# Five per-token stages as two merged half-batch chunks, context keys made once, expert rows added in DRAM

## The chip, the core and the metric

The kernel runs on one core of a Trainium2 chip. The metric is the device time of one execution in microseconds (us), as the median of several runs. Engines: PE is TensorE, DVE is VectorE, ACT is ScalarE, POOL is GpSimd, SP is SyncE, which issues nearly all DMAs. Each engine runs its own static list of instructions, and semaphores join them.

## The reference

The input is x (4 batches, 1024 tokens, 256 wide) and a context of 77 rows per batch. Eight stages follow, each added to x, most after a layer norm:

```
L0 attention on the context (differential, two softmaxes), then L0 block:
   own causal attention (16 heads of 16), then the best 2 of 8 experts per token
   (256 -> 1024, gelu, 1024 -> 256), weighted by a softmax over the two gates
C1 attention on the context, 16 heads of 16, with output projection
L1 ternary weights, 8-bit activations:
   xq = clip(round(x * (127 / max|x|)));  gelu(xq @ W1q.T + b1) quantised again, @ W2q.T + b2
D2 attention on the context, with biases and output projection
L2 butterfly block:  x @ W_exp, butterfly (linear), + bias, gelu, butterfly, @ W_con
E3 attention on the context, some context rows masked, no output projection
F3 a router takes 4 of 16 heads (64 wide) by the mean of all 1024 tokens of the batch,
   self attention with these, output projection
```

C1, L1, D2, L2 and E3 work on each token alone (the 77 context rows are fixed for a batch). F3 needs all tokens of a batch.

## The kernel before

Everything lives on one core in four parts. A **preamble** splits weights into high and low float16 halves and multiplies the butterfly factors into two dense matrices. **Phase 0** runs batches 0 to 3 unrolled through L0 attention, own attention and the gate; at its end POOL notes each token's place in the experts' table (L1595). **Phase 1** runs the experts in 23 tiles of 512 gathered rows. POOL gathers the normalised rows of a tile (L1610), the tile's results are stored in order to `scr_expert_rows`, and `final_slots` on DVE (L2079 to L2088) works out for every token where its two results lie. Then `add_expert_rows` on POOL (L1617) gathers 16 times 128 rows and adds them to `h_tokens` (L1622). **Phase 2** is a loop of four passes, one per batch (`Fori` at L673 on SP, L1112 on PE, L1464 on ACT, L1632 on POOL, L2130 on DVE). A pass first makes the context keys KX and values VX of its batch for C1, D2 and E3 (ACT L1470/L1473, DVE L2138/L2140), then does C1, L1, D2, L2, E3 and F3 one after the other, each over all 1024 tokens, and POOL adds the next batch's expert rows in the middle of the pass.

The order of the work inside an attention is a hand-written list, `context_attention_steps` (L115; `unprojected_steps` L146 for E3), which every engine walks through: S scores to find the row maximum (PE L923, DVE L1886), MT maxima turned (PE L934), ST scores turned with the maximum subtracted (PE L948) and exponentials on ACT (L1357), PV products with the values and a row of ones (PE L965), RINV and NB for the inverse sums, output projection in three parts WS, WB, WL (`split3` L763 to L765, three matmuls for one product in split float16). The path has several trips by DMA: the queries go to `scr_q` and come back as `q_stack` (L563, L568), the maxima as rows (L541), the sums of the probabilities out to another layout and, inverted on DVE (L1909), back (L548, L550), after which NB (L978) spreads them with a matmul and DVE multiplies (L1913). The ternary stage has per 128 tokens a matmul up (L1138, L1142), `hidden` on DVE (L2170), gelu on ACT (L1487), `quantise` on DVE (L2176 to L2190) with ACT L1493, transposes and ACT L1498, a matmul down (L1150, L1155) and two operations on DVE (L2194, L2197). The butterfly stage has L1174 up, gelu on ACT (L1513), L1183 down. `claim()` gives a matmul one of the PSUM slots: A0, A1 (large), B0, B1, S0, S1.

Of the kernel before, what the change touches and what calls it, by code (L numbers as in the profile page):

```python
# [7 lines left out]
P = 128  # L8
# [20 lines left out]
NP, NPX = 5, 7  # L29
# [10 lines left out]
FLAT = ["A0q", "A0o", "B0q", "B0k", "B0v", "C1q", "D2q", "E3q"]  # L40
PADDED = ["B0p", "C1o", "D2o", "F3o"]
# [73 lines left out]
def context_attention_steps():  # L115

    def S(g, a, b):
        return [("S", g, t) for t in range(a, b)]

    def ST(g, a, b):  # L120
        return [("ST", g, 0, j) for j in range(a, b)]

    def PV(g):
        return [("PV", g, 0, 0), ("PV", g, 0, 1)]

    steps = S(0, 0, NT) + [("MT", 0)] + S(1, 0, NT) + [("MT", 1)]
    for j in range(GH):
        steps += ST(0, j, j + 1) + S(2, 2 * j, 2 * j + 2)
    steps += [("MT", 2)]
    for g in range(NG):  # L130
        for j in range(GH if g + 1 < NG else 0):
            if j == 3:
                steps += PV(g)
            steps += ST(g + 1, j, j + 1) + (S(3, 2 * j, 2 * j + 2) if g == 0 else [])
        if g == 0:
            steps += [("MT", 3)]
        if g == NG - 1:
            steps += [("WS", 0)] + PV(g)
        else:
            steps += [("RINV", g)]  # L140
        if g:
            steps += [("NB", g - 1)]
    return steps + [("RINV", NG - 1), ("WS", 1), ("WB", 0), ("WB", 1), ("NB", NG - 1), ("WS", 2), ("WB", 2), ("WL",)]


def unprojected_steps():  # L146

    steps = [("TO", s[1]) if s[0] == "NB" else s for s in context_attention_steps()]
    return [s for s in steps if s[0] not in ("RINV", "WS", "WB", "WL")]


def attention_steps(L, route=False):
    if L == "E3":
        return unprojected_steps()
    return own_attention_steps(route) if L == "B0" else context_attention_steps()
# [24 lines left out]
def build(nc, A, out, known, stages):  # L180
    led = Ledger(known)
    with ExitStack() as ctx:
# [55 lines left out]
        maskr = sb("mask_row", [1, TX], I32)  # L238
# [6 lines left out]
        def area(kb, n, dt=F32, rows=P):  # L245
# [5 lines left out]
        stage_pad = area(32, len(PADDED) * PAD_N)  # L251
# [8 lines left out]
        kxs = area(40, 2 * 3 * KD * TX, F16).rearrange("p (s l k c) -> p s l k c", s=2, l=3, k=KD)  # L260
        kxf = area(44, 3 * KD * TX).rearrange("p (l k c) -> p l k c", l=3, k=KD)
        CT = area(47, 2 * KD * TX, F16).rearrange("p (s k c) -> p s k c", s=2, k=KD)
        maskb = area(56.5, NH * TX, F16, rows=1).rearrange("p (h c) -> p h c", h=NH)
        tmp = area(60, T)
        XN = {k: area(o, NT * D).rearrange("p (t d) -> p t d", d=D) for k, o in
              {"A": 48, "B": 16, "M": 38, "C": 16, "D": 16, "E": 16, "L1": 16, "L2": 16, "F": 28}.items()}
        VP = area(0, NT * NH * QUARTER).rearrange("p (t h d) -> p t h d", h=NH, d=QUARTER)
        PR = area(16, NP * T).rearrange("p (n c) -> p n c", c=T)
        PRX = area(8, NPX * T).rearrange("p (n c) -> p n c", c=T)
        OT = {True: [area(36 + 4 * (g % 2), T) for g in range(NG)],  # L270
              False: [area(36, T), area(40, T), area(0, T), area(4, T)]}
# [38 lines left out]
        slots_u = area(63.5, 2 * NT * NB).bitcast(U32)  # L310
# [6 lines left out]

        b1b = area(0, HID)
        hb = area(4, 3 * HID).rearrange("p (n c) -> p n c", n=3)
        xq = area(24, NT * D, F16).rearrange("p (t d) -> p t d", d=D)  # L320
        xqT = area(28, KD * T, F16).rearrange("p (k c) -> p k c", k=KD)
        hq = area(32, 2 * HID, F16).rearrange("p (n c) -> p n c", n=2)
        hqT = area(36, 2 * HID, F16).rearrange("p (n c) -> p n c", n=2)
        b2b = area(40, D)
        hr = area(44, 2 * HID).rearrange("p (n c) -> p n c", n=2)

        XTf = area(0, KD * T).rearrange("p (k c) -> p k c", k=KD)
        gT = area(24, 2 * NM * CH).rearrange("p (n m c) -> p n m c", n=2, m=NM)

# [2078 lines left out]
```

## Time and profile before

| what | value |
|---|---|
| median of 3 runs | 4590.6 us (4576.54, 4590.60, 4591.11) |
| profiled execution | 4634.11 us, its span 4632.3 us |
| busy, share of the span | PE 72%, DVE 52%, PE weight loads 39%, ACT 31%, POOL 8% |
| mean granted TensorE clock | 0.808 of full speed |
| phase 2 begins | 2210.7 us |
| passes | four |

The profiled execution is one run; the windows and timelines below have its time, counted from the start of its span. Busy time of an engine counts its instructions, without the issue of DMAs and waits for semaphores. The granted clock is that of TensorE alone, as a fraction of 2.4 GHz. In a timeline, the number in brackets is how long the engine was idle before the row, and what ended the idle time; "x16" is sixteen instructions in a row.

### The profile page before, as it was taken

Reading aid. Unit: us, or ns where it says so; the run is one execution under the profiler, and the core shown is the slowest. Engines: PE = TensorE matmul, PEld = TensorE weight load, DVE = VectorE, ACT = ScalarE, POOL = GpSimd, SP = SyncE. Lnnn points to the kernel's source line nnn. Section 1 sums busy time; section 2 is a strip of 40 time slices with the busy share of each in tenths; the row PEclk is TensorE's granted clock in tenths of the full one; section 3 lists DMA queues with packets and bytes.
Section 4 is the critical chain, followed back from the end, with each engine's and each line's share of the span. In section 5 each row is a group of like instructions: output and inputs, shape, how many; then the busy total and the mean of one; then the engine's idle time right before and its main releaser. Section 6 shows DMA issues by size and latency. Waiting matters only on the chain.

```text
span 4632.3 us, 49203 instructions
## 1 busy us (share of the span) xinstructions
PE 3357.5 (72%) x18898; PEld 1800.3 (39%) x18898; DVE 2394.3 (52%) x4963; ACT 1452.2 (31%) x2041; POOL 370.6 (8%) x287
## 2 busy tenths in 40 slices
PE   5278677677677579997558596585966777856769
PEld 2132332332332256675335333353333453433524
DVE  8765465465465345554563443634437434365343
ACT  2234433433333323332242323332224332233222
POOL 6000001001001112112020000200002000020000
PEclk7677777777768889998769797687887788877889
DMA  3210311311221044443320303201131112131110
GB/s 123 98 38 15 120 33 15 109 44 15 92 61 15 29 160 140 139 137 100 59 48 5 72 2 67 50 10 31 46 65 36 25 24 53 42 58 26 24 53 24
DMA packets 186166, 266.56 MB, mean 58 GB/s; under 512 B 86985, under 2 KB 132570, under 8 KB 173530
## 3 DMA queue, kind: packets, MB, share of 16 engines
q1 hardware_dynamic: 167934, 240.61, 19.1%
q0 software_dynamic: 17984, 22.63, 2.8%
q8 instruction: 157, 2.57, 0.2%
q14 instruction: 91, 0.75, 0.1%
HBM read 185.37 MB, written 75.33 MB: 56 GB/s over the span
## 4 chain that ended last, share of the span: by engine, by line
PE 52%; DVE 27%; DMA 8%; ACT 5%; issue 4%; SPq 2%; another core or an unknown queue 1%; POOL 1%; DVEq 0%; ACTq 0%; POOLq 0%
PE ps L763 6%; PE ps L764 5%; PE ps L765 5%; PE ps L965 5%; PE ps L1251 4%; PE ps L948 4%; DVE max_parts L1880 4%; PE ps L910 3%; PE ps L1174 2%; PE ps L1183 2%; DVE minus_max L1886 2%; PE ps L978 2%; DMA q_stack<-scr_q 2%; DVE arena L1799 2%; ACT arena L1357 2%
## 5 line engine op out<-in xcount | busy, mean ns | idle before, releaser
L1357 ACT ACTIVATE arena<-ps 104x1024 f32<-104x1024 f32 (+8 forms) x704 | 514.1, 752 | 838.0 <-PE ps L948 602.1
L1880 DVE TENSOR_REDUCE max_parts<-ps 128x1 f32<-128x512 f32 (+3 forms) x768 | 389.3, 552 | 258.4 <-PE ps L913 160.3
L910 PE MATMUL ps<-k_stack,q_stack 96*128 96x512 f16 (+3 forms) x768 | 277.4, 397 | 94.1 <-DVE max_parts L1880 50.3
L1797 DVE CAST arena<-arena 128x512 f16<-128x512 f32 (+2 forms) x304 | 161.5, 531 | 332.4 <-ACT arena L1440 222.6
L948 PE MATMUL ps<-q_stack,k_stack 98*128 98x512 f16 (+3 forms) x768 | 265.3, 393 | 37.2 <-ACT arena L1357 22.8
L1622 POOL DMA_INDIRECT h_tokens<-scr_expert_rows,slots_of_batch x80 | 127.0, 1587 | 1915.6 <-DMA slots_of_batch<-scr_slots 1832.2
L1799 DVE TENSOR_TENSOR arena<-arena 128x512 f16<-128x512 f32 (+2 forms) x304 | 274.5, 903 | 10.4
L763 PE MATMUL ps<-arena 128*128 128x256 f16 (+2 forms) x824 | 223.0, 275 | 72.0 <-DVE arena L2133 70.6
L2273 DVE TENSOR_REDUCE max_parts<-ps 128x1 f32<-128x512 f32 x256 | 171.4, 689 | 184.5 <-PE ps L1226 182.4
L1251 PE MATMUL ps<-arena 128*96 128x512 f32 x512 | 246.1, 592 | 1.7 <-ACT arena L1558 1.7
L1558 ACT ACTIVATE arena<-ps 128x1024 f32<-128x1024 f32 x128 | 130.5, 1023 | 345.8 <-PE ps L1240 345.8
L821 PE MATMUL ps<-identf,arena 128*128 128x128 f32 x512 | 114.6, 415 | 170.2 <-DVE arena L1780 170.2
L1440 ACT ACTIVATE arena<-ps,arena 128x512 f32<-128x512 f32 x184 | 126.4, 687 | 355.2 <-PE ps L765 311.1
L764 PE MATMUL ps<-arena 128*128 128x256 f16 (+2 forms) x824 | 223.7, 274 | 0.0
L765 PE MATMUL ps<-arena 128*128 128x256 f16 (+2 forms) x824 | 223.3, 274 | 0.0
L910 PEld LDWEIGHTS ps<-k_stack,q_stack 96*128 96x128 f16 x768 | 77.3, 104 | 337.6 <-DVE max_parts L1880 247.9
L763 PE MATMUL ps<-x_channels_hi_lo,arena 128*128 128x512 f16 x432 | 168.4, 390 | 52.7 <-DVE arena L2260 49.1
L965 PE MATMUL ps<-arena 128*32 128x512 f32 (+3 forms) x1536 | 186.8, 571 | 13.7 <-ACT arena L1357 13.7
L923 PE MATMUL ps<-k_stack_context,q_stack 96*128 96x104 f16 x768 | 77.8, 288 | 145.2 <-DMA q_stack<-scr_q 141.4
L1595 POOL DMA_INDIRECT scr_taken<-v_context,slots_of_batch x64 | 61.5, 961 | 1443.4 <-DVE slots_of_batch L2034 1425.1
L821 PEld LDWEIGHTS ps<-identf,arena 128*128 128x128 f32 x512 | 102.2, 222 | 179.3 <-DVE arena L1780 129.3
L764 PE MATMUL ps<-x_channels_hi_lo,arena 128*128 128x512 f16 x432 | 168.3, 390 | 0.0
(406 smaller groups left out, 7057.1 us busy)
## 6 DMA issues: line engine op xcount, KB each, us to landing
arena<-scr_expert_weights SPq DMA_DIRECT2D x46, 1024.0 KB, 5.9
scr_q<-arena SPq DMA_DIRECT2D x40, 512.0 KB, 4.2
q_stack<-in_exp_W SPq DMA_DIRECT2D x16, 1024.0 KB, 8.3
scr_expert_weights<-k_stack SPq DMA_DIRECT2D x16, 1024.0 KB, 4.9
q_stack<-scr_q SPq DMA_DIRECT2D x60, 256.0 KB, 6.1
scr_expert_rows<-q_stack SPq DMA_DIRECT2D x23, 512.0 KB, 2.9
k_stack<-scr_q SPq DMA_DIRECT2D x36, 256.0 KB
scr_k<-arena SPq DMA_DIRECT2D x16, 512.0 KB, 4.4
```

Source lines behind the costliest of these rows:

```text
L763: pe.matmul(o, left[0], right[0], start=first, stop=False, **kw)
L764: pe.matmul(o, left[0], right[1], start=False, stop=False, **kw)
L765: return pe.matmul(o, left[1], right[0], start=False, stop=last, **kw)
L821: mm = pe.transpose(s[:, k * CH + t % 4 * P:k * CH + (t % 4 + 1) * P], XN[N][:, t, k * P:(k + 1) * P], identf[:])
L910: mm = pe.matmul(s[:, 0:n], QS[0:MROW, buf, j, t * P:(t + 1) * P], KS[0:MROW, buf, j, c * CH:c * CH + n], start=True, stop=not on_edge)
L948: mm = pe.matmul(o, key_rows, q_stack[0:MROW + 2, buf, j, a:(c + 1) * CH], start=True, stop=not edge)
L965: mm = pe.matmul(acc[c][QUARTER * j:QUARTER * (j + 1), a - c * CH:CH], v, p, start=kt == 0, stop=final, tile_position=(0, QUARTER * j))
L1251: pe.matmul(acc[c][0:TV], VP4[:, kt, h, :], PR4[:, (h * NT + kt) % NP, c * CH:(c + 1) * CH], start=kt == 0, stop=kt == NT - 1).then_inc(*d ...
L1357: act.activation(probs[0:rows, n % np_, kt * P:T], slot(L, "ST", g, kt, j)[0:rows, kt * P:T], ACT.Exp).then_inc(*did("act", L, "exp", g, k ...
L1799: dve.tensor_tensor(lo, src, hi, ALU.subtract).then_inc(*step(*key))
L1880: dve.tensor_reduce(mpart[:, j * NT + t, c:c + 1], slot(L, "S", g, t, j, c)[:, 0:n], AX, ALU.max).then_inc(*frees("dve", L, "S", g, t, j, c))
L2273: dve.tensor_reduce(mpart[:, t, c:c + 1], slot("F3", "S", h, t, c), AX, ALU.max).then_inc(*frees("dve", "F3", "S", h, t, c))
```

## The change

Phase 2 takes the 1024 tokens as two chunks (c = 0, 1) of 512. `chunk_steps(c)` writes down the steps of all five stages for a chunk with a planned time for each; chunk 1 is LAG = 27.0 us behind. `chain_steps` sorts the two lists by planned time, and each engine walks through the one merged list. So chunk 1's C1 stands beside chunk 0's ternary stage, and so on. Nearly all buffers exist twice, by chunk; the PSUM slots S0, S1, B0, B1 become one ring "SB". The ring `hb` for the ternary hidden rows is 2 deep per chunk (3 before, for all).

Inside a context attention the inverse sums no longer travel by DMA: PE transposes the PV result (TO, 8 transposes for two head groups), DVE inverts and multiplies, PE transposes back (BK), and the output projection (W) takes 6 + 2 matmuls per 128 tokens in place of 14. Scores take 77 columns, not 104.

```diff
+TCH = CH // P
+LAG = 27.0
-FLAT = ["A0q", "A0o", "B0q", "B0k", "B0v", "C1q", "D2q", "E3q"]
-PADDED = ["B0p", "C1o", "D2o", "F3o"]
+FLAT = ["A0q", "A0o", "B0q", "B0k", "B0v", "C1q", "D2q", "E3q", "C1o", "D2o"]
+PADDED = ["B0p", "F3o"]
+def chunk_steps(c):
+    steps, now = [], [LAG * c]
...
+        for p in range(2):
+            for g in (2 * p, 2 * p + 1):
+                for t in range(TCH):
+                    add(0.6, "S", L, c, g, t)
+            add(0.8, "MT", L, c, p)
+        for kind, *i in (("ST", 0, 0), ("ST", 0, 1), ("ST", 1, 0), ("PV", 0), ("ST", 1, 1), ("ST", 2, 0), ("PV", 1), ("TO", 0), ("ST", 2, 1),
+                         ("ST", 3, 0), ("PV", 2), ("ST", 3, 1), ("PV", 3), ("TO", 1)):
+            add({"ST": 1.1, "PV": 0.9, "TO": 1.6}[kind], kind, L, c, *i)
+        if L != "E3":
+            add(3.5, "BK", L, c)
+            add(1.4, "W", L, c, 0)
+            add(2.0, "W", L, c, 1)
...
+    def butterfly():
+        norm("L2", c)
+        add(3.0, "T", "L2", c)
+        for m in range(NM):
+            add(1.75, "G", "L2", c, m)
+        for t in range(TCH):
+            add(3.5, "Y", "L2", c, t)
+
+    context_attention("C", "C1")
+    ternary()
+    context_attention("D", "D2")
+    butterfly()
+    context_attention("E", "E3")
+    norm("F", c)
+    add(0.0, "T", "F", c)
+    return steps
+
+def chain_steps():
+    return [step for at, step in sorted(chunk_steps(0) + chunk_steps(1), key=lambda s: s[0])]
```

The context keys and values of all four batches are made once, at the end of phase 0 (`context_keys`, on PE, ACT and DVE), and stored. Batch 0's are loaded by `load_keys` in phase 1. In each pass, after E3's last PV, SP loads the next batch's, ahead of the loads of the weights that F3's router has selected:

```diff
+            def load_keys(kx, vx, mask):
+                for n, s in enumerate((0, 1, 0)):
+                    sp.dma_start(KX[16 * n:16 * n + 16, :, :, 0:TC].rearrange("i l h c -> i (l h) c"),
+                                 kx[s].rearrange("n p c -> (n p) c").rearrange("(h i) c -> i h c", i=DH)).then_inc(*did("ld_kx", "k", n))
+                sp.dma_start(KX[48:49, 2, :, 0:TC], mask).then_inc(*did("ld_kx", "mask"))
+                sp.dma_start(VX[0:TC, :, :, 0:DH].rearrange("c l h d -> c (l h) d"), vx.rearrange("c l (h d) -> c (l h) d", d=DH)).then_inc(*did("ld_kx", "v"))
...
+                for step in chain:
+                    chain_step(*step)
+                    if step == ("W", "C1", 1, 1):
+                        sp.wait_ge(*of("dve", "C1", "x", 1, 1))
+                        load_tokens(d_s[1:][bs], did("ld_next", 0)[0])
+
+                sp.wait_ge(*of("pe", "E3", "PV", 1, NG - 1))
+                load_keys(d_kx[1:][bs].rearrange("o s n p c -> (o s) n p c"), d_vx[1:][bs].rearrange("o c l d -> (o c) l d"), d_mask[1:][bs])
```

In phase 1 POOL adds each tile's results straight onto the tokens' rows in DRAM, four accumulating scatters of 128 rows per tile, one tile's after the other's. `scr_expert_rows`, `final_slots` and the gathers of `add_expert_rows` go. SP's load of table i + 4 waits until the rows of tile i are added, and after the last tile the first batch's rows are loaded in one plain DMA.

```diff
+            def add_rows(i):
+                pool.wait_ge(*of("dve", "y", i, TC4 - 1))
+                if i:
+                    pool.wait_ge(*of("st_y", i - 1, TC4 - 1))
+                for c in range(TC4):
+                    pool.indirect_dma_start(d_s.rearrange("b t d -> (b t) d"), bass.IndirectOffsetOnAxis(ap=taken[i % 4][:, c, 0:1].bitcast(U32), axis=0),
+                                            yt[:, i % 2, c], None, compute_op=ALU.add).then_inc(*did("st_y", i, c))
```

How the order moves, first on ACT where the ternary stage begins. Before, the last attention rows (L1369), then the norm's root and the ternary stage by itself:

```order
L1369 ACTIVATE arena<-ps 128x512 x2
L1294 ACT_TABLE_LOAD
L1294 ACTIVATE ln_std<-ln_mean_var,eps_zero_minus_magic 128x8
L1482 ACTIVATE arena<-ps 128x1024 x2
L1487 ACT_TABLE_LOAD
L1487 ACTIVATE arena<-arena 128x1024 x2
L1493 ACTIVATE arena<-arena,eps_zero_minus_magic 128x1024
L1498 ACTIVATE arena<-ps 128x1024
L1487 ACTIVATE arena<-arena 128x1024
L1493 ACTIVATE arena<-arena,eps_zero_minus_magic 128x1024
```

Now, at the same point of chunk 0 (L1493 is chunk 1's exponential, L1499 its PV copy, L1511 chunk 0's gelu, L1517 and L1523 its quantised rows):

```order
L1499 ACTIVATE arena<-ps 128x512
L1511 ACT_TABLE_LOAD
L1511 ACTIVATE arena<-arena 128x1024
L1493 ACT_TABLE_LOAD
L1493 ACTIVATE arena<-ps 77x1024 x2
L1499 ACTIVATE arena<-ps 128x512
L1511 ACT_TABLE_LOAD
L1511 ACTIVATE arena<-arena 128x1024
L1517 ACTIVATE arena<-arena,eps_zero_minus_magic 128x1024
L1493 ACT_TABLE_LOAD
L1493 ACTIVATE arena<-ps 77x1024
L1523 ACTIVATE arena<-ps 128x1024
```

Chunk 1's exponentials stand between chunk 0's gelus, with a table load at each change. A pass has 13 table loads before and 34 now.

On DVE in the ternary stage. Before, one tile follows the other (L2170 hidden, L2176 to L2190 quantise, L2194 and L2197 output):

```order
L2181 TENSOR_SCALAR small_work<-small_work,ternary_scales 128x1
L2183 TENSOR_SCALAR small_work<-small_work 128x1
L2187 TENSOR_SCALAR arena<-arena,small_work 128x1024
L2190 TENSOR_SCALAR arena<-arena 128x1024
L2194 SCALAR_TENSOR_TENSOR x_tokens<-ps,small_work,x_tokens 128x256
L2197 TENSOR_TENSOR x_tokens<-x_tokens,arena 128x256
L1766 BN_STATS ln_stats<-x_tokens 128x6
L2170 SCALAR_TENSOR_TENSOR arena<-ps,small_work,arena 128x1024
```

Now, towards the end of chunk 1's ternary stage (L2178 and L2181 are its output, L2069 to L2082 its quantise, L2117 the score maxima of chunk 0's D2):

```order
L2117 TENSOR_REDUCE minus_max_context<-ps 128x4 x2
L2178 SCALAR_TENSOR_TENSOR x_tokens<-ps,small_work,x_tokens 128x256
L2181 TENSOR_TENSOR x_tokens<-x_tokens,weights_flat 128x256
L2040 BN_STATS ln_stats<-x_tokens 128x6
L2117 TENSOR_REDUCE minus_max_context<-ps 128x4 x2
L2069 TENSOR_REDUCE small_work<-arena 128x1
L2071 TENSOR_SCALAR small_work<-small_work 128x1
L2073 RECIPROCAL small_work<-small_work 128x1
L2074 TENSOR_SCALAR small_work<-small_work,ternary_scales 128x1
L2076 TENSOR_SCALAR small_work<-small_work 128x1
L2080 TENSOR_SCALAR arena<-arena,small_work 128x1024
L2082 TENSOR_SCALAR arena<-arena 128x1024
```

The maxima of the other chunk's next attention are taken in among the tiles.

On ACT in the butterfly stage now (L1528 is a gelu of the butterfly, L1493 an exponential and L1499 a PV copy of the other chunk; before, the 16 gelus of the stage follow one table load without another between them):

```order
L1528 ACT_TABLE_LOAD
L1528 ACTIVATE arena<-ps,up_bias_whole 128x512
L1493 ACT_TABLE_LOAD
L1493 ACTIVATE arena<-ps 77x1024
L1528 ACT_TABLE_LOAD
L1528 ACTIVATE arena<-ps,up_bias_whole 128x512
L1493 ACT_TABLE_LOAD
L1493 ACTIVATE arena<-ps 77x1024
L1499 ACTIVATE arena<-ps 128x512
L1528 ACT_TABLE_LOAD
```

Each gelu of 512 columns has a table load before it, and so has the next exponential.

## Rows read from the trace of the kernel before

**Rows 1.** The page: the chain that ended last, its share by engine
```profile
PE 52%; DVE 27%; DMA 8%; ACT 5%; issue 4%; SPq 2%; another core or an unknown queue 1%; POOL 1%; DVEq 0%; ACTq 0%; POOLq 0%
```

**Rows 2.** Windows of the first pass, stage by stage; the line above names the columns
```profile
core 0: us, PE busy (x) PEld busy (x) DVE busy (x) ACT busy (x) POOL busy (x), PEclk, DMA share, GB/s
2210.00:2220.00 10.00, 6.61 (x58) 5.43 (x58) 1.99 (x4) 4.60 (x11) 0.00 (x0) 0.62 0.65 158
2220.00:2309.00 89.00, 58.09 (x396) 34.27 (x396) 50.04 (x99) 28.47 (x33) 0.00 (x0) 0.83 0.25 39
2309.00:2378.00 69.00, 34.17 (x176) 18.59 (x176) 57.43 (x136) 29.96 (x29) 25.39 (x16) 0.65 0.32 57
2378.00:2466.00 88.00, 59.77 (x396) 34.86 (x396) 47.71 (x92) 27.18 (x31) 0.00 (x0) 0.81 0.18 33
2466.00:2534.00 68.00, 63.28 (x240) 42.79 (x240) 10.96 (x46) 16.22 (x22) 0.00 (x0) 0.95 0.00 0
2534.00:2605.00 71.00, 43.49 (x300) 23.89 (x300) 37.89 (x83) 27.07 (x31) 0.00 (x0) 0.77 0.22 39
2605.00:2612.00 7.00, 3.65 (x16) 3.28 (x16) 6.04 (x12) 3.33 (x3) 0.00 (x0) 0.50 0.00 0
2612.00:2629.00 17.00, 0.93 (x10) 0.77 (x10) 4.70 (x24) 1.81 (x7) 0.00 (x0) 0.50 0.21 46
```

**Rows 3.** Timeline of SP: the first DMA of the second pass
```profile
2813.34 0.35 SPq L675 DMA_DIRECT2D q_stack<-in_c_qs  x1
```

**Rows 4.** Timeline of VectorE in the ternary stage: two successive tiles' first operation
```profile
2340.26 1.28 DVE L2170 SCALAR_TENSOR_TENSOR arena<-ps,small_work,arena 128x1024 f32<-128x1024 f32 x1 [0.30 <-PE ps L1142]
...
2345.99 1.27 DVE L2170 SCALAR_TENSOR_TENSOR arena<-ps,small_work,arena 128x1024 f32<-128x1024 f32 x1
```

**Rows 5.** Timeline of TensorE in the butterfly stage
```profile
2471.55 28.70 PE L1174 MATMUL ps<-arena,butterflied_W_exp 128*128 128x512 f32 x64
2500.09 3.62 PE L1183 MATMUL ps<-butterflied_W_con_turned,arena 128*128 128x256 f32 x16
```

**Rows 6.** Timeline of TensorE in context attention
```profile
2246.23 3.24 PE L923 MATMUL ps<-k_stack_context,q_stack 96*128 96x104 f16 x32 [11.73 <-DMA q_stack<-scr_q]
...
2290.25 1.98 PE L978 MATMUL ps<-arena,spread_sums 128*128 128x512 f32 x4
2292.07 0.27 PE L763 MATMUL ps<-weights_padded,arena 128*128 128x256 f16 x1
2292.18 0.27 PE L764 MATMUL ps<-weights_padded,arena 128*128 128x256 f16 x1
...
2586.53 1.04 PE L972 MATMUL ps<-identf,arena 128*128 128x128 f32 x8
```

**Rows 7.** Timeline of ScalarE: a table load and the gelu behind it
```profile
2472.83 1.28 ACT L1513 ACT_TABLE_LOAD   x1
2474.54 0.69 ACT L1513 ACTIVATE arena<-ps,up_bias_whole 128x512 f32<-128x512 f32 x1 [0.42 <-PE ps L1174]
```

**Rows 8.** Timeline of VectorE and GpSimd around the experts
```profile
1622.24 0.96 POOL L1595 DMA_INDIRECT scr_taken<-v_context,slots_of_batch  x1 [0.30 <-issue]
...
1717.73 0.95 POOL L1610 DMA_INDIRECT x_tokens<-scr_x_normalised,arena  x1 [0.30 <-issue]
...
2171.33 1.66 DVE L2074 TENSOR_SCALAR q_stack<-ps,arena 128x256 f32<-128x256 f32 x4 [2.86 <-PE ps L1082]
2210.69 0.79 DVE L2131 TENSOR_SCALAR arena<-mask_row 1x1232 f16<-1x1232 int32 x1 [37.70 <-SPq L498]
...
2193.20 1.54 POOL L1622 DMA_INDIRECT h_tokens<-scr_expert_rows,slots_of_batch  x1 [2.51 <-DMA h_tokens<-scr_expert_rows,slots_of_batch]
```

**Rows 9.** DMA issues of the page: size of one, microseconds from issue to landing
```profile
arena<-scr_expert_weights SPq DMA_DIRECT2D x46, 1024.0 KB, 5.9
scr_q<-arena SPq DMA_DIRECT2D x40, 512.0 KB, 4.2
...
q_stack<-scr_q SPq DMA_DIRECT2D x60, 256.0 KB, 6.1
```

More of the change, by code:

```diff
@@ L146, in unprojected_steps, with add, norm, context_attention @@
[L146 to L155, printed above, removed]
+def chunk_steps(c):
+    steps, now = [], [LAG * c]
+    def add(us, *step):
+        steps.append((now[0], step))
+        now[0] += us
+    def norm(N, c):
+        add(2.0, "LN", N, c)
+        add(3.0, "XN", N, c)
+    def context_attention(N, L):
+        norm(N, c)
+        add(3.5, "T", N, c)
+        add(1.5, "Q", L, c, 0)
+        add(2.0, "Q", L, c, 1)
+        add(1.0, "LD", L, c, 0)
+        add(4.0, "LD", L, c, 1)
+        for p in range(2):
[10 more added lines that the diff above has]
+            add(2.0, "W", L, c, 1)
+    def ternary():
+        norm("L1", c)
+        add(5.0, "XQ", "L1", c)
+        start = now[0]
+        for kind, t, at in (("H1", 0, 0.0), ("H1", 1, 1.4), ("QZ", 0, 2.8), ("H1", 2, 5.0), ("QZ", 1, 6.4), ("HR", 0, 6.4), ("HQ", 0, 7.4), ("H1", 3, 8.6),
+                            ("H2", 0, 8.8), ("QZ", 2, 10.0), ("HR", 1, 10.0), ("HQ", 1, 11.0), ("H2", 1, 12.4), ("QZ", 3, 13.6), ("HR", 2, 13.6),
+                            ("HQ", 2, 14.6), ("H2", 2, 16.0), ("HR", 3, 17.2), ("HQ", 3, 18.2), ("H2", 3, 19.6)):
+            now[0] = start + at
+            add(2.0, kind, "L1", c, t)
+    def butterfly():
[13 more added lines that the diff above has]
+    return steps
@@ L533, in max_rows @@
                 n = NT if L == "F3" else GH * NT
-                stack = KS if L in XL and g >= 2 else QS
                 for s in range(2):
@@ L898, in attention @@
                         buf = g % 2
-                        q_stack = QS if own or g < 2 else KS
-                    if kind == "S" and own:
+                    if kind == "S":
                         t, j = step[2:]
@@ L1187, in _ @@
[L1187 to L1195 removed]
+                for step in chain:
+                    chain_step(*step)
                 s = claim("S", "F", "R")
@@ L1945, in attention @@
                 last = None
-                for i, s in enumerate(steps):
+                for s in own_attention_steps(led.batch > 0):
                     if s[0] == "S":
-                        last = maxima(L, own, s)
+                        last = maxima(L, s)
                     elif s[0] == "MT":
-                        minus_max_rows(L, s[1], last, GH * NT if own else 0)
+                        minus_max_rows(L, s[1], last, GH * NT)
                         minus_max_parts(L, s[1], GH * NT)
@@ L2219, in _ @@
-                statistics("E", X, NT - 1, ("L2", "x"))
-                norm("E", X, XN["E"])
-                x_lo("E")
-                attention("E3", False, X, "F")
-                norm("F", X, XN["F"])
-                x_lo("F")
+                for step_ in chain:
+                    chain_step(*step_)
                 def small_step(key, ins):
```

1016 lines of the change are left out of this document (543 added, 473 removed).

## The prediction

> **What bounds the kernel now.** I first read the chain of waits by engine [rows 1]: 52% TensorE, 27% VectorE, 8% DMA, 5% ScalarE. No engine bounds the whole, so it has to be read by stage, in the windows of the first pass [rows 2]. The reader should look in each row for the engine that is full. In C1 (89 us) TensorE is busy for 58.1 and VectorE for 50.0; they take turns. In the ternary stage (69) VectorE is at 57.4 and TensorE at 34.2. In D2 (88) it is as in C1. In the butterfly stage (68) TensorE is at 63.3 with a granted clock of 0.95 and VectorE nearly idle at 11.0. In E3 (71) nobody is full: 43.5 and 37.9. Keys before it (10) and the norm behind it (7) complete the 402 us from 2210 to 2612 that the change rebuilds. Four engines' half-filled stages beside each other are what a merge can use; a full engine it can't shorten. The second pass starts at 2813.3 [rows 3], so a pass is 603 us, and the 201 behind 2612 (selection of heads, F3) keep their code.
>
> **The merged chain, by its full engine.** I cut a pass of the merged list into five stretches.
>
> a) Start to the norm of chunk 0's ternary stage. Chunk 0 works alone for most of it. Half of C1's 89 would be 44.5, but trips don't halve: the wait for the query stack is 11.7 [rows 6], with a store of 4.2 and a load of 6.1 in it [rows 9], and I add 2 for small handoffs: (89 − 14)/2 + 14 = 51.5. Chunk 1's entry disturbs it: 55.
>
> b) Both ternary stages. VectorE takes a new tile each 5.73 us with no idle time between (2340.26 and 2345.99, [rows 4]); eight tiles and the entries are the 57.4 of the window. Into the same stretch fall the end of chunk 1's C1 (9 of the 25 that half of C1's 50.0 is) and the front half of chunk 0's D2 (half of half of 47.7, 12, and 0.6 for small operations): 57.4 + 9 + 12.6 = 79. With handoffs in a fixed order, 88. TensorE has about 34 + 30 there and waits.
>
> c) Back half of chunk 0's D2 beside chunk 1's front: one chunk's attention of TensorE time. From C1's 58.1, half is 29.0. Out go the spreading matmuls L978, four per chunk, 1.98 for four, and 6 of 14 output matmuls per 128 tokens, which start 0.11 apart (2292.07 to 2292.18): 4 × 6 × 0.11 = 2.6. In come 24 transposes at 1.04 for eight: 3.1. The scores of a head group cost 3.24 for the batch, so 6.5 per chunk for four groups, and if their time goes with the columns (77 for 104) 1.7 of it goes. 29.0 − 2.0 − 2.6 + 3.1 − 1.7 = 26 (all rows in [rows 6]). With a little waiting: 28.
>
> d) Both butterfly stages, beside one chunk's attention. TensorE: 28.7 for the upward products and eight times 3.62 and bias downward [rows 5] are the 63.3 of the window; with 26, 89. TensorE should be nearly full: 92.
>
> e) Rest of chunk 1's E3 behind chunk 0, and the norm: (71 − 14)/2 + 14 = 42.5, + 7 = 49.5; 53 with handoffs.
>
> 55 + 88 + 28 + 92 + 53 = **316** in place of 402: 86 less per pass, 344 in four. The bare sums, 51.5 + 79 + 26 + 89 + 49.5, make 295; that is the lower end.
>
> **Table loads.** A pass has 34 in place of 13, because exponentials and gelus alternate on ScalarE. One takes 1.28, 21 × 1.28 = 27 us more of ScalarE [rows 7]. I cost them at nothing beyond the handoffs: in stretch d ScalarE has 16.2 of butterfly work, 13.6 of half an attention and 14 loads, 18: 48 of 92, and TensorE is the cover. Behind the load at 2472.83 ScalarE stood idle for 0.42, and TensorE ended that. So whatever else that switch cost is within 0.42. The Trainium skill (ScalarE: Activation LUTs, "What ACT_TABLE_LOAD costs") gives a load of 1283 ns and then a drain of about 1380 ns; the first number agrees with the row, the second finds no room in it. By that rule the result would be that of rival 3.
>
> **Smaller edits.** The keys' 10 per pass are in the 402 and go. At the end of phase 0 they come in once: four batches at some 6.6 of TensorE [rows 2], partly beside the 20 us in which GpSimd notes the last places (16 rows at 0.96 + 0.30, the last at 1622.24, [rows 8]): +10, between 0 and 26. After the last tile, VectorE was idle for 37.7 until the pass began [rows 8]. Now four adds (at 1.54 + 0.30 for the like gathers, 7.4), their landing (2.51, [rows 8]) and a load of 1 MB (5.9, [rows 9]) with handoffs come to 24: −14. `final_slots` and some of the preamble: −6. `load_keys` is queued on SP ahead of the selected weights, which fall in a window of 17 where all engines wait [rows 2]. The trace has no such small pieces; bounds are 0 (landed while the router works) and 7 per pass, a little over the 6.1 of a stack [rows 9]: 0 to +28, I take +10, nearer to nothing since the router's chain covers the start. The load of the next rows after C1 has hundreds of us to land. Sum of all this: 0.
>
> Adding in DRAM puts a wait into each tile: an add waits for the tile's last y and for the previous tile's add, and the next pick is queued behind it on GpSimd. A tile is 22.6 us; picks take 4 × (0.95 + 0.30) = 5.0 [rows 8], adds 7.4, landing 2.5. 15 of 22.6: hidden; I price it at nothing.
>
> **The number.** Against the profiled execution: 4634.1 − 344 = 4290. The median of the runs shown lies 43 below that execution, so from 4590.6: **4247**.
>
> **Rivals.**
> 1. The waits vanish too (0.13): the trips of stretch a and e hide behind the other chunk, 285 per pass, 117 less than 402. For it: 14 us of a and of e are pure waits. Against: nothing of chunk 1 stands beside the start. Result 4590.6 − 4 × 117 = 4123.
> 2. The fixed order makes chunks wait (0.17). In ScalarE's queue a gelu of chunk 0 stands behind exponentials of chunk 1, which wait for TensorE, which waits for a slot that chunk 0's VectorE work frees. Eight tiles at 3 us more (a table load and an exponential with its handoff) are 24 in b; 12 in d; 10 in the rest: 362 per pass, 4431. For it: the order rows on ScalarE; the planned times put the end at 245 us, below what VectorE alone allows in b, so the order is drawn for a chain faster than any there can be. Against: a wait in one chunk leaves the other's steps only until the queue's head.
> 3. A switch of tables costs a second load's 1.28 (0.06), and ten of the switches in d lie on the path, where gelus feed the downward products: 13 a pass, 52 in all, 4299. Against: the 0.42 of [rows 7]. That is what the drain of the Trainium skill's page (ScalarE: Activation LUTs) would do.
> 4. Slower, by the clock (0.03): if TensorE stayed at its lower level, 1.2 GHz, through the chain. Its busy time in the six windows from 2220 to 2612 is 262; weighted with each window's clock it is 214, so at full clock I take about 222, near the lower end since clock and work coincide. At half speed: 444, 42 more than 402, +168: 4759. It turns slower when the mean clock of the chain is below 222/402 = 0.55. The clock was 0.65 to 0.95 in stages with gaps [rows 2], and gaps shrink.
> 5. The adds pace the experts (0.03): each scatter has to read and write in DRAM. At 30 us per tile, 23 × 7.4 = 170: 4417; slower than before from 38 us per tile.
> That the change does not do what it says is excluded by the order lists, in which every engine has both chunks' steps mixed.
>
> **Chances and range.** The forecast (295 to 340 per pass, 4163 to 4343) has 0.58. The range has to reach most of rivals 1 and 2: 4105 to 4405, which leaves out the upper part of rival 2 and rivals 4 and 5. A measurement of this kernel tells 0.3% (14 us) from no change. Slower by more: rival 4 and a third of rival 5, 0.04; within: 0.01; faster: 0.95.
>
> **What would show it.** SP's first DMAs of two passes are about 517 apart (603 − 86). VectorE is busy over 90% from chunk 0's first ternary tile to chunk 1's last (b); TensorE about 95% in d, with a clock above 0.85 over the chain. 34 table loads per pass at 1.28, none with a gap of its own. Tile pace still 22.6, idle time from phase 1 to phase 2 at most 25. It is wrong if the chain is as long as 340 or more with neither engine above 85% in b or d: then the order makes the waits (rival 2), and ScalarE's or VectorE's rows have long waits on the other chunk; or if the tile pace has moved (rival 5).

## The result, and the profile after

The changed kernel took 4607.0 us (median of 8 runs) beside 4589.5 for the kernel before (8 runs): a ratio of 1.0037, 95% interval 1.0025 to 1.0049. It is slower by 17 us, where 343 us less had been forecast. The profiled execution has a span of 4601.8 us. That of the kernel before [rows 1 to 9] lay 44 us above its median, so the kernel before was profiled a second time below. The kernel before took 4590 us in some sets of runs and 4625 in others, even on one and the same chip, so ratios are taken within a set; the surplus lies ahead of phase 2 (of the changed kernel and its variants, phase 2 begins at 2177 to 2180 in profiles of the first kind of set and at 2205 to 2217 in those of the second), so the lengths of passes are compared across sets.

The page of the changed kernel, busy time by engine and the chain by engine [rows 1]:

```profile
PE 3400.6 (74%) x18770; PEld 1790.8 (39%) x18770; DVE 2294.0 (50%) x4977; ACT 1587.0 (34%) x2186; POOL 391.3 (9%) x298
...
PE 52%; DVE 26%; ACT 9%; DMA 5%; issue 4%; SPq 2%; POOL 1%; DVEq 0%; ACTq 0%; another core or an unknown queue 0%; POOLq 0%
```

DMA has left the chain as meant (8% to 5%), and ScalarE has come in (5% to 9%). TensorE is busy for 43 us longer with fewer matmuls. Where a pass begins, in SP's timeline [rows 3]:

```profile
2176.89 0.36 SPq L739 DMA_DIRECT2D q_stack<-in_c_qs  x1
...
2782.76 0.35 SPq L739 DMA_DIRECT2D q_stack<-in_c_qs  x1
```

The first pass is 605.9 us and the mean of three 605.8; before, the first was 602.6 and the mean of three 606.9. So the merged chain has saved nothing that can be seen. The windows of the first pass, cut where the five stretches of the prediction end (the norm's root on ScalarE of chunk 0's L1, chunk 1's D, chunk 0's L2, chunk 1's E and chunk 1's F), beside [rows 2]:

```profile
core 0: us, PE busy (x) PEld busy (x) DVE busy (x) ACT busy (x) POOL busy (x), PEclk, DMA share, GB/s
2177.00:2249.00 72.00, 45.89 (x267) 25.10 (x267) 30.97 (x83) 20.02 (x24) 0.00 (x0) 0.60 0.30 59
2249.00:2356.00 107.00, 62.51 (x380) 35.98 (x378) 78.14 (x193) 52.72 (x54) 0.00 (x0) 0.70 0.11 23
2356.00:2398.00 42.00, 30.23 (x182) 16.76 (x180) 16.51 (x42) 16.59 (x20) 0.00 (x0) 0.72 0.19 33
2398.00:2506.00 108.00, 90.35 (x441) 56.54 (x442) 31.19 (x86) 46.42 (x53) 0.00 (x0) 0.94 0.07 13
2506.00:2577.00 71.00, 47.92 (x222) 21.19 (x219) 26.64 (x67) 29.43 (x35) 0.00 (x0) 0.56 0.21 25
```

Every stretch is 14 to 19 us longer than forecast: 72, 107, 42, 108 and 71 are 400, for a forecast of 316 and 402 before. The busy times of the fullest engines were read right: VectorE has 78.1 in b (79 expected), TensorE 90.4 in d (89). What is off is the rest, in which no engine is full: VectorE is at 73% in b, TensorE at 84% in d, and in a and e the clock is down at 0.60 and 0.56.

### The profile page after: what moved, and what is told of

It reads as the page before. It is cut to its first block, busy times and chain, and to the rows that moved or that the text cites. A ratio compares the mean times of both kernels' runs of the same rounds, so it can differ in the third digit from the quotient of the medians.

```text
span 4601.8 us, 49189 instructions
## 1 busy us (share of the span) xinstructions
PE 3400.6 (74%) x18770; PEld 1790.8 (39%) x18770; DVE 2294.0 (50%) x4977; ACT 1587.0 (34%) x2186; POOL 391.3 (9%) x298
## 4 chain that ended last, share of the span: by engine, by line
PE 52%; DVE 26%; ACT 9%; DMA 5%; issue 4%; SPq 2%; POOL 1%; DVEq 0%; ACTq 0%; another core or an unknown queue 0%; POOLq 0%
PE ps L806 5%; PE ps L807 5%; PE ps L808 5%; PE ps L1323 5%; DVE max_parts L1973 4%; PE ps L986 3%; PE ps L1117 3%; PE ps L948 3%; PE ps L1187 2%; DVE minus_max_context L2117 2%; PE ps L969 2%; ACT arena L1493 2%; PE ps L1180 2%; PE ps L1126 2%; PE ps L1079 2%
## 5 line engine op out<-in xcount | busy, mean ns | idle before, releaser
L1425 ACT ACTIVATE arena<-ps 128x256 f32<-128x256 f32 (+7 forms) x512 | 321.5, 650 | 480.3 <-PE ps L969 294.0
L1893 DVE CAST arena<-arena 128x512 f16<-128x512 f32 (+2 forms) x296 | 144.3, 488 | 365.3 <-ACT arena L1588 235.6
L969 PE MATMUL ps<-q_stack,k_stack 98*128 98x512 f16 (+3 forms) x768 | 258.9, 385 | 37.8 <-ACT arena L1425 22.6
L1895 DVE TENSOR_TENSOR arena<-arena 128x512 f16<-128x512 f32 (+2 forms) x296 | 239.0, 807 | 10.2
L1493 ACT ACTIVATE arena<-ps 77x1024 f32<-77x1024 f32 x192 | 189.9, 1016 | 109.7 <-PE ps L1109 109.3
L806 PE MATMUL ps<-x_channels_hi_lo,arena 128*128 128x512 f16 x432 | 167.9, 389 | 52.6 <-DVE arena L2382 48.9
L807 PE MATMUL ps<-arena 128*128 128x256 f16 (+1 forms) x752 | 205.9, 274 | 0.0
L808 PE MATMUL ps<-arena 128*128 128x256 f16 (+1 forms) x752 | 205.9, 274 | 0.0
L806 PE MATMUL ps<-arena 128*128 128x256 f16 (+1 forms) x752 | 205.7, 274 | 0.0
L2132 DVE RECIPROCAL inverse_sums_by_token<-ps 128x32 f32<-128x32 f32 x48 | 17.1, 356 | 354.1 <-PE ps L1126 354.1
L1117 PE MATMUL ps<-arena,v_context 77*32 77x512 f32 x768 | 147.7, 850 | 52.9 <-ACT arena L1493 52.9
L1715 POOL DMA_INDIRECT scr_x<-q_stack,arena x92 | 151.6, 1648 | 258.3 <-DVE q_stack L2302 237.3
L2117 DVE TENSOR_REDUCE minus_max_context<-ps 128x4 f32<-128x308 f32 x384 | 155.2, 464 | 26.5 <-PE ps L1095 26.5
```

The costliest lines, as they stand in the source:

```text
L806: pe.matmul(o, left[0], right[0], start=first, stop=False, **kw)
L807: pe.matmul(o, left[0], right[1], start=False, stop=False, **kw)
L808: return pe.matmul(o, left[1], right[0], start=False, stop=last, **kw)
L969: mm = pe.matmul(o, KS[0:MROW + 2, buf, j, kt * P:(kt + 1) * P], QS[0:MROW + 2, buf, j, a:(c + 1) * CH], start=True, stop=not edge)
L1117: mm = pe.matmul(s[QUARTER * j:QUARTER * (j + 1)], VX[0:TC, XL.index(L), g * GH + j, :], PRc[c][:, (2 * g + j // 2) % 3, j % 2], start=Tru ...
L1425: act.activation(PR[:, n % NP, kt * P:T], slot(L, "ST", g, kt, j)[:, kt * P:T], ACT.Exp).then_inc(*did("act", L, "exp", g, kt, j))
```

## Experiments

**1. The kernel before, profiled again.** No edit.

> The kernel before, unchanged, profiled a second time, since its profiled execution lay 44 us above its median and the two traces can't be compared stage by stage to 20 us. If the four passes took 603 to 607 us each in that execution by chance, they are shorter here; if the surplus lies elsewhere (phase 0 of that execution is 25 to 30 us longer than the changed kernel's, though its list there is the same), the passes stay at 603 to 607 and phase 2 begins near 2182.

Measured: span 4625.5, first pass from 2201.0 to 2806.6, 606.8 on the mean of three. The passes are as long as in the first profile, so some 607 us is their length. Phase 2 begins at 2201, only 10 us earlier than in the first profile and not near the 2182 that was expected. Its timelines, GpSimd's first note of a place for the last batch and VectorE's first result row of the experts:

```profile
1593.17 0.96 POOL L1595 DMA_INDIRECT scr_taken<-v_context,slots_of_batch  x1 [111.29 <-DVE slots_of_batch L2034]
...
1673.86 0.87 DVE L2074 TENSOR_SCALAR q_stack<-ps,arena 128x256 f32<-128x256 f32 x2
```

The same two places, and the way into phase 2 [rows 8], of the changed kernel:

```profile
1562.43 1.26 POOL L1689 DMA_INDIRECT scr_taken<-v_context,slots_of_batch  x1 [103.33 <-DVE slots_of_batch L2262]
...
1669.53 0.87 DVE L2302 TENSOR_SCALAR q_stack<-ps,arena 128x256 f32<-128x256 f32 x2
...
2176.85 1.41 DVE L2090 BATCH_NORM_STATS2 ln_stats<-h_tokens 128x6 f32<-128x256 f32 x4 [15.46 <-SPq L534]
```

From the first note to the first result row it is 107.1 us instead of 80.7: the context keys cost 26 there, not 10. Into phase 2 VectorE is idle for 15.5 us instead of 37.7: 22 saved, not 14. Together +4, where these two had been put at −4 (and the sum with `final_slots`, the preamble and `load_keys` at 0). From the first note to the end of the execution it is 3039.4 us in the changed kernel, and 3029.0 and 3032.3 in the two profiles of the kernel before: 7 to 10 of the 17 us lie there. Where the rest lies these rows don't show.

**2. The chunks one after the other, and farther apart.**

```diff
-LAG = 27.0
+LAG = 1000.0
```

> LAG = 1000: the two chunks' steps no longer mix; chunk 1 starts its C1 when chunk 0 has left E3. This measures what one chunk of 512 tokens costs alone. Theory A (in-order queues: each chunk waits for the other's unready steps, alone it would be quick): one chunk takes about 200 to 215 us alone, a chain of 400 to 430, total 4600 to 4720. Theory B (one chunk's own dependent steps are long, whatever stands between them; the merge hides much and that just pays for the halving): 250 to 265 alone, a chain of 500 to 530, total 5000 to 5120. Theory C (TensorE's clock): the mean granted clock in the chain is below the 0.70 that the merged chain shows, with the same steps in TensorE taking up to twice as long.

Measured: ratio 1.1023 (1.0987 to 1.1060), a pass of 721.8, 116 more than with the merge. Theory B has it. The first chunk's C1, L1, D2, L2 and E3, windows of this kernel:

```profile
core 0: us, PE busy (x) PEld busy (x) DVE busy (x) ACT busy (x) POOL busy (x), PEclk, DMA share, GB/s
2207.00:2269.00 62.00, 39.47 (x190) 19.61 (x190) 18.64 (x43) 16.61 (x19) 0.00 (x0) 0.55 0.21 43
2269.00:2308.00 39.00, 17.59 (x88) 9.46 (x88) 29.25 (x75) 16.76 (x17) 0.00 (x0) 0.65 0.00 0
2308.00:2370.00 62.00, 38.91 (x190) 19.12 (x190) 18.89 (x45) 16.66 (x20) 0.00 (x0) 0.56 0.13 22
2370.00:2408.00 38.00, 34.03 (x120) 21.30 (x120) 5.06 (x16) 9.14 (x12) 0.00 (x0) 0.91 0.00 0
2408.00:2459.00 51.00, 29.58 (x150) 13.04 (x150) 17.73 (x47) 15.52 (x18) 0.00 (x0) 0.59 0.15 27
```

Half the tokens cost much more than half the time in the attentions: 62 of C1's 89 and 51 of E3's 71. The part that does not halve is 2 × 62 − 89 = 35 us, not the 14 of the prediction (31 by E3). The 89 is from the old code with its trips by DMA and the 62 from the new code, as in the prediction's own sum, so this isn't the price of halving alone; no run has the new code on all 1024 tokens. In these windows the clock is 0.55 to 0.59, where it was 0.77 to 0.83 with all 1024 tokens [rows 2]. Theory C's clock is there too: 0.62 over the chunk. With the norm behind E3, a chunk of 512 costs 260 alone, and two would cost 520. The merge with 27 gets 120 of that back, about what the halving loses.

With LAG = 55:

> LAG = 55 in place of 27, the planned length of one context attention: chunk 1's whole C1 stands beside chunk 0's ternary stage. Theory A (27 makes conflicts): the pairing of a VectorE stage with attention is better, 10 to 30 us less per pass, total 4490 to 4570. Theory B: more of the pass has a chunk alone (28 us more at the start and at the end, half of it regained): 10 to 30 more per pass, 4650 to 4730.

Measured: ratio 1.0137 (1.0104 to 1.0170), a pass of 618.8, 13 more than with 27. That is theory B again: what pairs in the middle does not pay for the longer stretches with one chunk.

**3. The table loads.**

```diff
-act.activation(hb[c][:, t % 2], hb[c][:, t % 2], ACT.Gelu)
+act.activation(hb[c][:, t % 2], hb[c][:, t % 2], ACT.Copy)
...
-act.activation(gT[c][:, m], slot("L2", "G", c, m)[:, 0:CH], ACT.Gelu, bias=upb[:, m:m + 1], scale=1.0)
+act.activation(gT[c][:, m], slot("L2", "G", c, m)[:, 0:CH], ACT.Identity, bias=upb[:, m:m + 1], scale=1.0)
```

> The gelus of the ternary and the butterfly stage are replaced by a copy and an identity with the same bias, so what is computed leaves the gelu out in these two stages. The same number and size of ACTIVATE instructions remain, in the same order, but 20 of the 34 table loads per pass go (14 stay). Theory D (the alternating table loads lie on the chain, at 1.28 each): 15 to 26 us less per pass, total 4500 to 4550. If they are covered, as the prediction had it: less than 4 us per pass, total above 4590.

Measured: ratio 0.9892 (0.9857 to 0.9926), a pass of 589.7: 16 us less, the lower edge of theory D (15 to 26). 20 loads gone are 0.8 us each, not the whole 1.28. The loads were costed at nothing, with TensorE as cover. The changed kernel's ScalarE at the start of the butterfly stretch:

```profile
2408.35 1.28 ACT L1528 ACT_TABLE_LOAD   x1
2409.64 0.69 ACT L1528 ACTIVATE arena<-ps,up_bias_whole 128x512 f32<-128x512 f32 x1
2410.35 1.28 ACT L1493 ACT_TABLE_LOAD   x1
2411.64 1.02 ACT L1493 ACTIVATE arena<-ps 77x1024 f32<-77x1024 f32 x1
2412.68 1.28 ACT L1528 ACT_TABLE_LOAD   x1
```

From 2408.35 to 2418.79 ScalarE has no gap of more than 0.02 us: it is the full engine there, and more than half of its time is loads. The share of 48 in 92 was an average over the stretch. A load takes 1.28 and the next function starts 0.01 later, so nothing like the drain of the Trainium skill (ScalarE: Activation LUTs, "What ACT_TABLE_LOAD costs") comes on top of it here: of the first pass's 34 loads 19 have the next function within 0.02, and the others are followed by a wait for another engine. Rival 3's condition, loads on the chain, was right. That its 13 us per pass come near the 16 measured is luck: its cause, a second load's time behind each switch, is not there; it is the load itself.

**4. Another order of the same steps.** Only the merge differs: each chunk's own order stays, and a string says whose step is next.

```diff
+MERGE = ('0001100001110000000101000000000111001011000101011010110001111011010110001011110100'
+         '0100101001000100010011000101001111011000111011111010110011000010010001000010010100'
+         '0101000111110101101111101111011101110101011011101010100010110011010010101111100100'
+         '1111100000100011100000010000000101111111001111101111011101001010110110101100111101')
 def chain_steps():
-    return [step for at, step in sorted(chunk_steps(0) + chunk_steps(1), key=lambda s: s[0])]
+    lists = [iter(sorted(chunk_steps(c), key=lambda s: s[0])) for c in range(2)]
+    return [next(lists[int(c)])[1] for c in MERGE]
```

> Only the merge of the two chunks' lists differs: each chunk's own order stays, but which chunk's step comes next is a string of 328 digits, found by a search that replays the list with the durations of the traces (TensorE's at 1.3 times those at full clock) and each engine strictly in order. Replayed so, the merge by planned times takes about 400 us per pass (413 at 1.39, where 401 were measured) and this one 340. Theory A (the fixed order makes steps of one chunk wait behind unready steps of the other, and much of the 400 is that): 40 to 60 us less per pass than the changed kernel, a ratio to the kernel before of 0.95 to 0.97, 22 table loads in a pass instead of 34. Theory E (the length comes from the steps' own durations, the clock above all, and no order mends it): less than 15 us per pass, ratio above 0.99.

Measured: 4305.7 us beside 4592.6, ratio 0.9367 (0.9340 to 0.9395). That is faster than both kernels. The first pass is 527.2, the second 535.4 and the third 532.6, 68 to 79 less than with the merge by planned times. Theory A has it, and by more than its 40 to 60. The five stretches in this kernel, cut at the same norms:

```profile
core 0: us, PE busy (x) PEld busy (x) DVE busy (x) ACT busy (x) POOL busy (x), PEclk, DMA share, GB/s
...
2180.00:2241.00 61.00, 42.79 (x294) 23.44 (x294) 34.42 (x88) 23.77 (x28) 0.00 (x0) 0.72 0.37 71
2241.00:2324.00 83.00, 54.41 (x335) 32.38 (x335) 72.95 (x182) 46.48 (x49) 0.00 (x0) 0.73 0.13 29
2324.00:2364.00 40.00, 33.66 (x241) 17.82 (x239) 22.03 (x55) 22.37 (x27) 0.00 (x0) 0.84 0.20 35
2364.00:2443.00 79.00, 75.36 (x342) 49.56 (x340) 21.78 (x59) 30.38 (x38) 0.00 (x0) 0.98 0.10 17
2443.00:2501.00 58.00, 44.90 (x276) 21.49 (x276) 31.77 (x83) 25.64 (x32) 0.00 (x0) 0.67 0.25 30
```

Their sum is 321, for a forecast of 316. VectorE is at 88% in b (the prediction's sign was over 90%), TensorE at 95% with a clock of 0.98 in d (about 95% was the sign); over the chain the clock is 0.79, not above 0.85. The stretches don't hold the same steps as in the changed kernel (342 matmuls in d, 441 there), so only the length of the whole compares. Some of the difference between the two orders shows in the waits of ScalarE (line <- releaser: us in total, times, longest), in the chain of the changed kernel:

```profile
ACT ln_std L1473 <- DVE ln_mean_var L2093: 94.5, 11, 23.0
```

and of this one:

```profile
ACT ln_std L1480 <- DVE ln_mean_var L2100: 30.6, 8, 10.9
```

The norm's root of a chunk, 0.3 us long, stands at the head of ScalarE's queue until VectorE has the chunk's variance. Such a wait costs when a ready step of the other chunk stands behind it. One place in the changed kernel where the rows show that, first a line of the chain of waits, then ScalarE's timeline:

```profile
2304.15 0.69 DVE arena L2082
...
2307.85 0.30 ACT L1473 ACTIVATE ln_std<-ln_mean_var,eps_zero_minus_magic 128x4 f32<-128x4 f32 x1 [4.92 <-DVE ln_mean_var L2093]
2308.05 1.13 ACT L1517 ACTIVATE arena<-arena,eps_zero_minus_magic 128x1024 f16<-128x1024 f32 x1
```

VectorE has done its part of quantising chunk 0's last ternary tile at 2304.8. ScalarE's step on that tile (L1517) starts only at 2308.05, since the root of chunk 1's norm (L1473) is ahead of it in the list, and TensorE, idle for 6.1 us, waits for L1517. VectorE is busy all the while, so this place shows the mechanism and not its price; how much of the 68 to 79 us is made of such waits was not added up. The longest wait for a root, ScalarE and then TensorE in the same 25 us:

```profile
2481.54 1.28 ACT L1473 ACT_TABLE_LOAD   x1
2505.78 0.30 ACT L1473 ACTIVATE ln_std<-ln_mean_var,eps_zero_minus_magic 128x4 f32<-128x4 f32 x1 [22.96 <-DVE ln_mean_var L2093]
```

```profile
2485.63 3.62 PE L1187 MATMUL ps<-butterflied_W_con_turned,arena 128*128 128x256 f32 x16
2489.52 0.99 PE L1095 MATMUL ps<-k_stack_context,q_stack 96*128 96x77 f16 x16
2491.04 0.70 PE L1095 MATMUL ps<-k_stack_context,q_stack 96*128 96x77 f16 x8 [0.53 <-DVE minus_max_context L2117]
2491.81 3.72 PE L1187 MATMUL ps<-butterflied_W_con_turned,arena 128*128 128x256 f32 x16
```

Chunk 0's scores for E3 (L1095) stand between chunk 1's downward products (L1187), 3.7 us each, and come through a few at a time. TensorE is nearly full there, but chunk 0's exponentials, the next in ScalarE's queue, become ready only at 2506, and ScalarE stands idle for 23 us. So here nothing ready stands behind the root, apart from a table load; it is the order in TensorE's list that brings chunk 0's exponentials so late. Afterwards both chunks are in E3 with TensorE at 0.56 of its clock. The last norm of chunk 0 is at 2537.8 and that of chunk 1 at 2576.9: for 39 us only one chunk is left. In the searched merge these are 2494.2 and 2500.9, 7 us apart, and chunk 1 starts 7 us behind chunk 0 and not 27.

**5. How much of it is the distance.**

```diff
-LAG = 27.0
+LAG = 8.0
```

> LAG = 8: both chunks are in the same stage nearly all the time, so only 14 table loads per pass remain, but stages with the same full engine stand beside each other. The searched merge also starts chunk 1 only 7 us behind chunk 0. If that early start were the gain: ratio below 0.96. If the gain is in the fine order of steps: 0.985 to 1.0, as the replay has it (13 us per pass less than with 27).

Measured: ratio 0.9752 (0.9717 to 0.9786, two runs), a first pass of 567.7, 38 less than with 27, and 14 table loads per pass. The chain is 368. The ratio lies between the two forecasts, and the gain is three times what the replay had (13), so the replay is a rough guide. Two fifths to a half of what the search found is had with one number (32 of 79 us in the chain, 38 of 79 in the first pass); the rest, 368 to 321, is the fine order. The gain from 27 to 8 can't be parted from the table loads by these runs: 20 loads fewer were 16 us in experiment 3.

**6. The table loads in the better order.** The edit of 3 on the kernel of 4.

> The searched merge, with the gelus of the ternary and butterfly stage replaced by copy and identity (the gelu is left out of what is computed): 12 table loads per pass in place of 22. In the planned merge taking 20 loads out gave 16 us per pass. If a load costs that wherever it stands (0.8 each): 8 us per pass, ratio near 0.930. If in this merge the loads stand where ScalarE has slack, which the search could see: under 3 us per pass, ratio 0.934 to 0.937.

Measured: ratio 0.9341 (0.9322 to 0.9361), passes of 529.5, 528.4 and 525.7. Against 0.9367 (0.9340 to 0.9395) in another set nothing can be told apart. A nearer comparison is the kernel of experiment 8, which ran in the same set, has the loads and differs otherwise only in one store ahead of phase 2: 4338.7 us there and 4322.0 here, 17 us apart, 8 of them ahead of phase 2. The passes are 531.1 and 527.9 in the mean, 3 us for 10 loads; with all 17 it would be 4. So the loads are nearly covered here: 0.3 to 0.4 us each. 1.28 us is no price by itself: the same kind of load cost 0.8 in one order and about half of that or less in another.

**7. TensorE's clock.** Extra matmuls, whose results the next matmul overwrites, where TensorE waits. Two of the five places are shown; the others are ahead of the maxima, the transposes of the PV result and the ternary input:

```diff
+            def warm(s, n):
+                for _ in range(n):
+                    pe.matmul(s[:, 0:CH], ident[:], Wq1[:, 0, 0:CH], start=True, stop=True)
...
                     s = claim("A", "T", N, c)
+                    warm(s, 12)
...
                     s = claim("SB", L, "S", c, g, t)
+                    if t == 0 and g == 0:
+                        warm(s, 12)
```

> The changed kernel with some 280 extra matmuls per pass (float16, 512 columns, written to the slot that the next matmul overwrites, so nothing of the result changes), placed where TensorE waits: before a chunk's transposes, its first scores, the maxima, the ternary input and the transposed results. At 0.22 us each at full clock they are 60 us of TensorE; it is idle for 124 of the chain's 401. Theory C (the chain's length follows TensorE's clock, mean 0.72 there against 0.79 in the kernel before): the mean granted clock of the chain rises above 0.85 and the time falls or stays within 10 us per pass in spite of the 60, since the matmuls on the chain take up to half as long. Without an effect of the clock: 20 to 50 us more per pass, 4700 to 4830.

Measured: ratio 1.0037 (1.0007 to 1.0066), the same as without them, passes of 608.5, 607.4 and 611.2. The window of the whole chain of this kernel:

```profile
2177.00:2587.00 410.00, 315.98 (x1764) 167.61 (x1764) 184.42 (x466) 165.33 (x184) 0.00 (x0) 0.85 0.16 28
```

The clock is 0.85 where it was 0.72, and TensorE is busy for 316 us, 39 more than the 277 without them. The 60 us that 280 matmuls take at full clock are an estimate from their 0.22 each; by it some 20 us were given back by faster matmuls. Theory C's forecast was met, but the run doesn't part what the clock gives from what the fillers cost: from the start of the pass to the last norm it is 9 us longer, the first pass 2.6.

On the kernel of experiment 4, with those two places only:

> The searched merge with some 190 extra matmuls per pass (float16, 512 columns, overwritten by the next matmul), ahead of the waits of TensorE for the normalised rows and for the loads of the queries, 40 us of TensorE at full clock. In the planned merge 60 us of such matmuls cost nothing in time and took the mean clock of the chain from 0.72 to 0.85. Theory C: here too the clock rises (chain 0.79 before) and the time stays within 0.5% of the searched merge, ratio 0.932 to 0.942. If TensorE is now the tighter engine, with 70 us idle in 321: ratio above 0.945.

Measured: ratio 0.9450 (0.9431 to 0.9470), passes of 539.9, 541.5 and 532.5. The clock of the chain rose to 0.89 and the time with it, by 13 and 6 us in the first two passes and by nothing in the third. The ratio lies at the lower edge of the second forecast (above 0.945), so TensorE seems to be the tighter engine now; what the higher clock alone is worth no run shows.

**8. The stores of the context keys.** On the kernel of experiment 4:

```diff
-                for row in ((n, NB) if n == 0 else (n,)):
+                for row in ((n, NB) if n == NB - 1 else (n,)):
...
-                        dve.wait_ge(*of(f"st_kx{n % 2}", n - 2 if n > 2 else NB, 1))
+                        dve.wait_ge(*of(f"st_kx{n % 2}", n - 2, 1))
```

> The searched merge, and the second copy of the context keys (a spare row for the load of the last pass) is stored with batch 3's keys and holds these, in place of right behind batch 0's. The result is the same. In the changed kernel VectorE stands idle for 21 us between batch 1's and batch 2's keys at the end of phase 0; the staging buffers are two deep, and batch 2 waits for two stores of batch 0 in pieces of 154 bytes. If these stores are the cause of the extra length there (107 us from the last notes to the first result rows, 81 before), the idle time falls by about 8 to 12 us and the total by as much, a ratio of 0.934 to 0.936; if it is the loads of the context weights, nothing moves.

The place in the changed kernel, between batches 1 and 2, first ScalarE, then VectorE:

```profile
1592.95 0.38 ACT L1466 ACTIVATE q_stack<-ps 77x256 f32<-77x256 f32 x1 [16.59 <-DMA scr_v_context<-q_stack]
...
1597.04 0.41 DVE L2033 CAST k_stack<-k_stack 128x462 f16<-128x462 f32 x1 [21.31 <-ACT k_stack L1461]
```

Measured: ratio 0.9375 (0.9357 to 0.9394), no change against 0.9367. The wait between batches 1 and 2 went (VectorE's step from one to the other is 5 us), but one of 18.4 now stands between batches 0 and 1, so the waiting has moved and not gone:

```profile
1625.15 0.40 DVE L2040 CAST k_stack<-k_stack 128x462 f16<-128x462 f32 x1 [18.39 <-ACT k_stack L1468]
```

That nothing moved was the forecast for the loads of the weights, but the profile does not show them there either, so neither theory stands. With the second store moved, ScalarE and TensorE wait there for things that the profile calls "remote" and "issue". From the first note to the first row it is 110.6 us here and 107.3 in the kernel of experiment 4. The 26 us of the keys are as much as four times the 6.6 of TensorE, but TensorE isn't what fills them: what ScalarE and VectorE wait for there is left open.

## Why the prediction was wrong

- **What bounds the kernel** and the busy times of the fullest engine in b and d were right: 79 forecast and 78.1 measured for VectorE in b, 89 and 90.4 for TensorE in d. In c TensorE was put at 26 and has 30.2, at a clock of 0.72.
- **The handoffs of the merged chain** are the step that failed. The bare sums were 295 and the allowance on top 21, put down as "with handoffs in a fixed order". Measured are 105. With another merge of the same steps it is 26 (321), so the order of the merge is what made the difference, and the sum can be had with a better one. That 321 lies so near 316 is partly luck: term a was put at 51.5 with chunk 0 alone, where a chunk alone takes 62, and the better order starts chunk 1 only 7 us behind. That the planned order was good enough was assumed in one sentence of rival 2: "a wait in one chunk leaves the other's steps only until the queue's head". An engine walks through one list; when its head waits, all behind it waits, both chunks' steps, as in the rows at 2304 to 2308 of experiment 4. Rival 2 had the mechanism and put the chain at 362, 46 above the forecast; measured are 84 above. The prediction's own sign of being wrong was met: a chain of 340 or more with neither engine above 85% in b or d, here 400 with 73% and 84%.
- **The part that does not halve** in (89 − 14)/2 + 14 was sized at 14 from the DMA trips alone and measures 35, by the same comparison of old code with new. Beside the trips there are dozens of short steps on alternating engines, and TensorE does its part at a clock of 0.55; how the 35 divide between these and the new code wasn't measured. This was also the term that hid the danger: with 260 per chunk, a poor merge loses all that the change can gain.
- **The table loads** were costed at nothing and cost 16 per pass, since their cover was taken as an average over the stretch. In the better order they are nearly covered.
- **Smaller edits**: keys +26 for +10 (the upper bound named was 26, and the allowance that part of it runs beside GpSimd's notes was not borne out), the way into phase 2 −22 for −14. `load_keys` costs nothing that can be seen, for +10: from chunk 1's last norm (2576.9) to the next pass (2782.8) is 206, and 209 in the second profile of the kernel before (2597.9 to 2806.6). The experts' tiles follow each other at 22.6 us in both kernels, with one step of 25.1 in the changed one, so the adds in DRAM are hidden, as forecast.
- **Rival 4** (clock) had the direction: 0.72 over the chain, 0.79 in the kernel before, far from its condition of 0.55. It fits with TensorE being busier with fewer matmuls. In experiment 7 the clock of 0.85 gave back an estimated 20 us per pass of TensorE's time; what of that lies on the chain was not measured.
- **The rest.** 4 × (605.8 − 606.9) and +4 are 0; 17 were measured, of which 7 to 10 are found behind the first note (experiment 1). The remainder of a difference of 0.4% is not resolved by these rows.

## What to carry to other kernels

When work is cut in chunks to be merged, first run the chunks one after the other: that shows what a chunk costs alone, and so how much the merge has to win before anything is gained. Then treat the merge as a thing to be searched: replay the list with measured durations and each queue strictly in order, and look whether the last chunk ends alone; here the same steps in another order were worth 7% (with 12 table loads fewer per pass). Take such a replay as a guide only: for LAG = 8 it had 13 us per pass less and 38 were measured. Price a table load, or any small extra, at the place where its engine is full, not by its share of a stretch.

## What the runs showed that had not been expected

An estimated 60 us per pass of extra matmuls in places where TensorE waited left the ratio at 1.0037 and made a pass 3 us longer in the mean, with the granted clock of the chain going from 0.72 to 0.85; an estimated 40 us of the same filler cost 0.8 to 0.9% (against the kernels of experiments 8 and 4) where the order was tight, although the clock rose there too, from 0.79 to 0.89. And C1 with half of its tokens, in the new code and with nothing beside it, ran at a clock of 0.55 where the whole stage in the old code had 0.83: there the chunk's matmuls were slower and its waits a larger share.
